# A decoder layer on one core: attention and expert stages joined in one block, row scores reordered, weight lows moved to VectorE, the routed tail sent by halves

## The chip, the cores and the metric

The kernel runs on one core of a Trainium2 chip. The metric is the device time of one execution in microseconds; the time of a kernel is the median over its runs. All times below come from one profiled execution, unless a median is named.

## What is computed

The input x has 8 sequences of 512 tokens with 256 features (4096 tokens in all), the context has 64 tokens per sequence. The layer does three things, each added to x:

```
x = x + mamba_like(layernorm(x))                 # its state input is constant: a fixed causal kernel
x = x + cross_attention(layernorm(x), ctx, ctx)  # 16 heads of 16, causal mask, softmax, output Wo
x = x + moe(layernorm(x))                        # shared MLP 256-1024-256 on all tokens, plus
                                                 # 8 experts of the same size, top 2 of 8 per token
```

The expert part in full:

```
shared = gelu(xf @ Wfc_s + bfc_s) @ Wproj_s + bproj_s
probs = softmax(xf @ Wr); keep the two largest, divide by their sum -> gate
routed = sum over e of (gelu(xf @ Wfc[e] + bfc[e]) @ Wproj[e] + bproj[e]) * gate[:, e]
```

## The kernel before, in words

The program is written by hand, engine by engine: each engine has its own list of instructions, which it takes strictly in order, and semaphores order them against each other. There are three blocks, and all engines meet at a barrier between two blocks. The first block is the mamba-like stage (to about 166 us). The second is attention (to about 371 us). The third holds the shared expert stage and the routed stage, which follow each other without a barrier.

A batch is one sequence: 512 tokens, four tiles of 128. A matmul in nearly full precision is three matmuls (`product`, lines 135 to 137): each operand is split into a high part (rounded by ScalarE) and a low part (whole minus high, `low`, line 141, on VectorE or GpSimd).

**Attention**, batch b of 8. For the softmax the row maxima are needed. `row_scores(b, t)` (L636) computes the scores of 128 queries for all heads into PSUM banks 4 and 5, and VectorE's `maxima(b, t)` (L903, L905) reduces them; as both banks are used for each tile, row scores t+1 wait for the maximum of t. `maxima_twice`, `transpose_maxima` (L656), `maxima_high` (ScalarE, L788) and `maxima_split` (VectorE, L914) bring the maxima into the layout of the keys. `key_scores(b, m)` (L664), for two halves m of the heads, computes transposed scores minus maxima; `exps` (ScalarE, L783) takes the exponentials; `weigh_values` (L682) sums them (L686) and weighs the values with them (L692). The sums are transposed (L696), inverted on VectorE (L919), spread over the features on ScalarE (L803) and transposed back (`spread_inverse`, L702); `divide` (VectorE, L924, L928) multiplies. Then `o_high` and `o_low` split the result, `project_o` (L709) multiplies by Wo, and `residual` (L935) adds to x. `project_q` (L627) makes the queries.

The work is pipelined over batches: while batch b has its key scores, batch b+1 has its row scores, batch b+2 its transposed input and queries, and batch b-1 its output projection. The order on TensorE is the loop at L739 to L766, that on VectorE L969 to L1007, that on ScalarE L826 to L849. The weights of the shared MLP are split here too: the high parts in four pieces on ScalarE (L839, batches 0 to 3), the low parts in two pieces on GpSimd (L871 to L875, beside batches 5 and 6 of its own list). GpSimd also computes the reciprocal standard deviations (L120, L122) and adds the bias of Wo to x (`add_bo`, L857 to L861). VectorE's normalisation of a batch (`apply_part`, L889 to L895) is four instructions.

**Shared stage**, batch b of 8: `transposes` (L1110), `logits` (L1130) and `transpose_logits` for the router, `choose` (VectorE, L1329) picks two experts by a chain of 14 short instructions, `ranks` counts the tokens before each, `place_rows`, `place_slots`, `place_gates` compute where a token's row goes, and GpSimd scatters the rows to DRAM (L1275). `up` (L1121) and `gelus` make the hidden layer, `lows` splits it, `down` (L1159) projects. TensorE's prologue for batch 0 is L1191 to L1198, then come whole batches. SP loads the router weights and biases at the start of the block (L1081 to L1084), GpSimd the weights of expert 0 (L1280).

**Routed stage**, blocks of 256 rows of one expert, 35 in the profiled execution: SP loads the rows, TensorE transposes, up and down, and at the end of a block VectorE adds the bias in both halves (`y`, L1633), multiplies both by the gate (L1638), and GpSimd adds both to the output by indirect transfers (L1599).

Of the kernel before, what the change touches and what calls it, by code (L numbers as in the profile page):

```python
# [18 lines left out]
def build(nc, d):  # L19
# [38 lines left out]
    with ctx:  # L58
# [110 lines left out]
        onesbd = ab("onesbd", [P, KD, PW])  # L169

# [391 lines left out]
        with ExitStack() as c:  # L562
# [18 lines left out]
            recs = used("recs", [P, KD, TB, P])  # L581
            causalT = tmp("causalT", [P, S])
            causalT16 = tmp("causalT16", [P, S], BF16)
            hTp_at = Place(hT_at)
# [6 lines left out]
                c, """b_hn_var b_hn_rstd b_hn_ready b_hT_psum b_hT_ready b_q_psum b_qT_ready b_bo_added b_n_psum  # L591
# [14 lines left out]
            with nc.Block() as block:  # L606
                @block.sync
                def _(sp):
                    sp.dma_start(selraw[:].rearrange("p m n -> p (m n)"), d["sel"]).then_inc(t_in, 16)
                    sp.dma_start(causalT[:], d["causalT"]).then_inc(t_in, 16)  # L610
                    sp.dma_start(fcraw[:], d["Wfc_s"].rearrange("(k p) e -> p k e", p=P)).then_inc(ws_in, 16)
                    sp.dma_start(prraw[:], d["Wproj_s"].rearrange("(k p) e -> p k e", p=P)).then_inc(ws_in, 16)

                @block.tensor
                def _(pe):
                    def transpose_x(b, i):
                        u = 2 * b + i
                        pe.wait_ge(hn_ready, TB * b + 2 * i + 2)
                        if u > 1:
                            pe.wait_ge(hT_ready, u)  # L620
                        for t in pair(i):
                            for k in range(KD):
                                last = nc.tensor.transpose(PS[:, x_bank(b, i), (k * 2 + t % 2) * P:(k * 2 + t % 2 + 1) * P],
                                                           hn[:, t, k * P:(k + 1) * P], ident[:])
                        last.then_inc(hT_psum, 1)

                    def project_q(b, m):  # L627
                        pe.wait_ge(hT_ready, 2 * b + 2)
                        if b:
                            pe.wait_ge(n_max, TB * b)  # L630
                        for k in range(KD):
                            last = product(PS[:, QB[m], :], [w[:, k, m * P:(m + 1) * P] for w in wqp],
                                           [x[:, k, :] for x in hTp], k == 0, k == KD - 1)
                        last.then_inc(q_psum, 1)

                    def row_scores(b, t):  # L636
                        i = TB * b + t
                        pe.wait_ge(qT_ready, KD * b + KD)
                        if i:
                            pe.wait_ge(n_max, i)  # L640
                        for m in range(KD):
                            for half in range(2):
                                rows = slice(half * P // 2, (half + 1) * P // 2)
                                at = PS[:, 4 + half, :].rearrange("p (i m n) -> p i m n", i=2, m=KD)[:, :, m, :]
                                last = nc.tensor.matmul(
# [3 lines left out]
                                if t and m == KD - 1:  # L649
                                    last.then_inc(n_psum, 1)  # L650
# [5 lines left out]
                    def transpose_maxima(b):  # L656
                        pe.wait_ge(mx_twice, b + 1)
                        if b > 1:
                            pe.wait_ge(x2_ready, 2 * (b - 1) - 1)
# [66 lines left out]
                    for m in range(KD):  # L726
                        project_q(0, m)
# [1014 lines left out]
```

## Time and profile before

| | us |
|---|---|
| median of 3 runs | 1019.85 (1019.09 to 1022.16) |
| the profiled execution, own time | 1017.67 |
| its span in the trace | 1015.8 |
| TensorE busy | 928.6 (91%), weight loads 794.4 (78%) |
| VectorE, ScalarE, GpSimd busy | 628.0 (62%), 556.8 (55%), 360.0 (35%) |
| mean granted TensorE clock | 0.982 of 2.4 GHz |
| chain that ended last, by engine | TensorE 58%, VectorE 2%, ScalarE 1%, transfers 1%, issue 1% |

The busy share is an average over stages with different limits. The chain that ended last names TensorE for most of what it covers. Where TensorE is busy all the time, only fewer or shorter matmuls would help; where it has gaps, the order of the work counts. The rows below are therefore read stretch by stretch.

### The profile page before, as it was taken

What the parts mean: (1) busy time and instruction counts of PE and PEld (TensorE: products, weight loads), DVE (VectorE), ACT (ScalarE), POOL (GpSimd) and SP (SyncE); (2) the same over time, 40 slices, a digit from 0 to 9 for tenths busy, and PEclk for the clock granted to TensorE, in tenths of its full rate; (3) what the DMA queues carried; (4) which work ended last, traced back from release to release, by engine and by line L of the source; (5) the groups of instructions that cost most, each with busy time, mean ns of one, the idle gap of its engine ahead of it and who ended that gap; (6) DMA issues with size and microseconds to landing.
All of it is one profiled execution on the core that took longest, in us unless ns stands there. A gap on an engine that the chain in (4) does not pass through costs nothing.

```text
span 1015.8 us, 20188 instructions
## 1 busy us (share of the span) xinstructions
PE 928.6 (91%) x6832; PEld 794.4 (78%) x6833; DVE 628.0 (62%) x1481; ACT 556.8 (55%) x1109; POOL 360.0 (35%) x325
## 2 busy tenths in 40 slices
PE   2998897789989767999999999999999999999995
PEld 2444696446556446888888989999999999999995
DVE  4898896766775537666665654656565655565552
ACT  2688752445445434555655456756576656566552
POOL 3641813221340016555555414323234332333222
PEclk9999899999999999999999999999999999999998
DMA  8200002000000012111112445422425242422322
GB/s 253 84 1 1 1 1 90 1 1 1 1 1 1 2 29 105 66 65 66 62 63 76 165 172 132 129 43 44 134 43 131 43 130 54 125 43 48 48 43 32
DMA packets 49312, 64.21 MB, mean 63 GB/s; under 512 B 10289, under 2 KB 42290, under 8 KB 49138
## 3 DMA queue, kind: packets, MB, share of 16 engines
q0 software_dynamic: 17504, 34.87, 14.5%
q1 hardware_dynamic: 31618, 27.68, 9.1%
q10 hardware_dynamic: 144, 1.05, 0.3%
q8 instruction: 28, 0.46, 0.2%
q14 instruction: 18, 0.15, 0.0%
HBM read 38.82 MB, written 24.77 MB: 63 GB/s over the span
## 4 chain that ended last, share of the span: by engine, by line
PE 58%; DVE 2%; ACT 1%; issue 1%; DMA 1%; SPq 0%; POOL 0%; DVEq 0%; POOLq 0%; ACTq 0%
PE PS L135 19%; PE PS L136 18%; PE PS L137 18%; PE PS L1525 2%; PE PS L1117 1%; DVE hidl L141 1%; DMA xr<-routed_rows 0%; ACT act L1214 0%; ACT hidh L1211 0%; PE PS L1142 0%; DVE wprl L141 0%; DVE wfcl L141 0%; POOL out_rows L1599 0%; PE PS L1151 0%; DMA wr<-in_Wr 0%
## 5 line engine op out<-in xcount | busy, mean ns | idle before, releaser
L1571 ACT ACTIVATE hideh<-PS,be 128x256 fp32r<-128x256 f32 x280 | 138.8, 496 | 148.1 <-PE PS L137 148.1
L1599 POOL DMA_INDIRECT out_rows<-y,toki x70 | 123.7, 1768 | 268.0 <-DVE y L1638 257.3
L141 DVE TENSOR_TENSOR hidel<-act32e,hideh 128x256 fp32r<-128x256 f32 x280 | 117.7, 425 | 95.6 <-ACT act32e L1573 95.3
L135 PE MATMUL PS<-xTeh,wfch 128*128 128x256 f32 x560 | 159.6, 285 | 1.2 <-issue 1.1
L137 PE MATMUL PS<-xTeh,wfcl 128*128 128x256 f32 x560 | 158.4, 283 | 0.0
L136 PE MATMUL PS<-xTel,wfch 128*128 128x256 f32 x560 | 158.4, 283 | 0.0
L135 PE MATMUL PS<-wprh,hideh 128*128 128x256 f32 x560 | 157.9, 282 | 0.0
L136 PE MATMUL PS<-wprl,hideh 128*128 128x256 f32 x560 | 154.9, 277 | 0.0
L137 PE MATMUL PS<-wprh,hidel 128*128 128x256 f32 x560 | 154.9, 277 | 0.0
L1573 ACT ACTIVATE act32e<-PS,be 128x256 f32<-128x256 f32 x280 | 139.0, 496 | 7.4 <-DVE hidel L141 7.0
L135 PEld LDWEIGHTS PS<-xTeh,wfch 128*128 128x128 f32 x560 | 107.2, 191 | 2.7 <-issue 1.9
L137 PEld LDWEIGHTS PS<-xTeh,wfcl 128*128 128x128 f32 x560 | 107.3, 192 | 0.0
L136 PEld LDWEIGHTS PS<-xTel,wfch 128*128 128x128 f32 x560 | 107.3, 192 | 0.0
L136 PEld LDWEIGHTS PS<-wprl,hideh 128*128 128x128 f32 x560 | 105.3, 188 | 0.0
L137 PEld LDWEIGHTS PS<-wprh,hidel 128*128 128x128 f32 x560 | 105.3, 188 | 0.0
L135 PEld LDWEIGHTS PS<-wprh,hideh 128*128 128x128 f32 x560 | 105.2, 188 | 0.0
L120 POOL TENSOR_TENSOR vare<-mv,small 128x4 f32<-128x4 f32 x24 | 9.5, 396 | 200.6 <-DVE mv L115 200.5
L1211 ACT ACTIVATE hidh<-PS,bfs 128x512 fp32r<-128x512 f32 x64 | 44.0, 688 | 59.4 <-PE PS L137 55.5
L1275 POOL DMA_INDIRECT routed_rows<-rows,slotc x64 | 67.2, 1050 | 24.6 <-issue 18.1
L135 PE MATMUL PS<-wpsh,hidh 128*128 128x256 f32 x256 | 73.5, 287 | 0.2 <-DVE hidl L141 0.2
L137 PE MATMUL PS<-wpsh,hidl 128*128 128x256 f32 x256 | 72.1, 281 | 0.0
L136 PE MATMUL PS<-wpsl,hidh 128*128 128x256 f32 x256 | 72.0, 281 | 0.0
(254 smaller groups left out, 2182.1 us busy)
## 6 DMA issues: line engine op xcount, KB each, us to landing
xr<-routed_rows SPq DMA_DIRECT2D x36, 272.0 KB, 2.7
fcraw<-in_Wfc POOLq DMA_DIRECT2D x8, 1024.0 KB
prraw<-in_Wproj POOLq DMA_DIRECT2D x8, 1024.0 KB
X<-in_x SPq DMA_DIRECT2D x8, 512.0 KB, 6.4
out_rows<-X SPq DMA_DIRECT2D x8, 512.0 KB, 3.0
routed_rows<-pads SPq DMA_DIRECT2D x8, 272.0 KB
out_rows<-y,toki POOLq DMA_INDIRECT x70, 3.8
ctx<-in_ctxT SPq DMA_DIRECT2D x4, 256.0 KB
```

The costliest lines, as they stand in the source:

```text
L120: nc.gpsimd.tensor_tensor(vare[:], mv[:, :, 1], eps4, ALU.add).then_inc(done, 1)
L135: nc.tensor.matmul(out, wh, xh, start=first, stop=False)
L136: nc.tensor.matmul(out, wh, xl, start=False, stop=False)
L137: return nc.tensor.matmul(out, wl, xh, start=False, stop=last)
L141: return eng.tensor_tensor(out, whole, high.bitcast(F32), ALU.subtract)
L1117: last = nc.tensor.transpose(PS[:, 4 + k, t * P:(t + 1) * P], hn[:, t, k * P:(k + 1) * P], ident[:])
L1211: nc.scalar.activation(hid[0][:, j, :], PS[:, j % 4, :], ACT.Gelu_apprx_tanh, bias=bfs[:, j:j + 1])
L1275: nc.gpsimd.indirect_dma_start(out=RG, out_offset=bass.IndirectOffsetOnAxis(ap=slotc[:, t, m:m + 1], axis=0), in_=rows[:, t, :], in_offset ...
L1525: last = nc.tensor.transpose(PS[:, 4, k * BLK + h * P:k * BLK + (h + 1) * P], xr[:, h, k * P:(k + 1) * P], ident[:])
L1571: nc.scalar.activation(hid[0][:, j, :], PS[:, j % 4, 0:BLK], ACT.Gelu_apprx_tanh, bias=bias)
L1573: nc.scalar.activation(act32[:, j % 2, :], PS[:, j % 4, 0:BLK], ACT.Gelu_apprx_tanh, bias=bias).then_inc(h_ready, 1)
L1599: nc.gpsimd.indirect_dma_start(out=out, out_offset=bass.IndirectOffsetOnAxis(ap=toki[:, h:h + 1], axis=0), in_=y[:, h, :], in_offset=None, ...
```

## The change

1. The attention stage becomes a set of functions that the last block calls: its engine lists stand in front of the shared stage's, in one block, and no barrier lies between them. The loops run over batches 0 to 6; batch 7 is written out among the shared prologue.
2. On TensorE, row scores 3 of batch b+1 stand behind `weigh_values(b)` (before: in front), `project_o(b-1, 0)` is cut into its two tiles with row scores, key scores and transposes between them, and `transpose_maxima` stands between the two `project_q`. `project_q(b, 0)` no longer waits for the maxima. ScalarE has `maxima_high` behind the spreads, between the two `evac_q`. VectorE has `invert_sums` in front of the normalisation and `residual(b-1, 0)` behind the second `x_low`.
3. The low parts of the shared MLP's weights are computed on VectorE, in four pieces of 1024 columns, behind `divide` of batches 1 to 4 (before: two pieces of 2048 on GpSimd).
4. At the end of a routed block the bias is multiplied by the gate first (`gated`), one instruction per half computes PSUM times gate plus that, and GpSimd sends each half when it is ready.
5. Many small tiles move so that they don't overlap with attention's; waits are added where tiles do overlap.

The diff, cut to its core (indentation changes left out):

```diff
+            def attention_tensor(pe):
                 def project_q(b, m):
                     pe.wait_ge(hT_ready, 2 * b + 2)
-                    if b:
+                    if m and b:
                         pe.wait_ge(n_max, TB * b)
-                def project_o(b, i):
+                def project_o(b, i, tiles=None, bank=YB):
                     pe.wait_ge(oT_ready, KD * b + KD)
-                    if u:
+                    if bank == YB:
                         pe.wait_ge(x2_ready, u)
-                    if i:
-                        pe.wait_ge(mx_ready, min(b + 3, B))
+                        pe.wait_ge(mx_ready, min(b + 2 + i, B))
...
-                for b in range(B):
+                for b in range(B - 1):
                     key_scores(b, 0)
                     row_scores(b + 1, 0)
                     transpose_x(b + 2, 0)
-                    project_o(b - 1, 0)
+                    project_o(b - 1, 0, [0])
                     row_scores(b + 1, 1)
                     key_scores(b, 1)
                     row_scores(b + 1, 2)
                     transpose_x(b + 2, 1)
-                    row_scores(b + 1, 3)
+                    project_o(b - 1, 0, [1])
                     weigh_values(b)
-                    transpose_maxima(b + 1)
+                    row_scores(b + 1, 3)
                     transpose_sums(b)
-                    for m in range(KD):
-                        project_q(b + 2, m)
+                    project_q(b + 2, 0)
+                    transpose_maxima(b + 1)
+                    project_q(b + 2, 1)
                     spread_inverse(b)
                     project_o(b - 1, 1)
-                for i in range(2):
-                    project_o(B - 1, i)
...
                 # ScalarE
                     evac_sums(b)
-                    maxima_high(b + 1)
                     evac_o(b)
                     for m in range(KD):
                         spread(b, m)
-                        evac_q(b + 2, m)
+                    evac_q(b + 2, 0)
+                    maxima_high(b + 1)
+                    evac_q(b + 2, 1)
...
                 # GpSimd
-                    if b in (5, 6):
-                        parts, whole = ((wfs, fcraw), (wps, prraw))[b - 5]
-                        low(nc.gpsimd, parts[1][:], whole[:], parts[0][:]).then_inc(ws_low, 1)
...
                 # VectorE
-                    residual(b - 1, 0)
                     stats_part(b + 3)
                     maxima(b + 1, 2)
                     x_low(b + 2, 1)
+                    residual(b - 1, 0)
                     maxima(b + 1, 3)
                     maxima_twice(b + 1)
+                    invert_sums(b)
                     for t in range(TB):
                         apply_part(b + 3, t)
                     maxima_split(b + 1)
-                    invert_sums(b)
                     divide(b)
+                    if 0 < b < 5:
+                        dve.wait_ge(ws_high, b)
+                        low(nc.vector, parts[1][:, part], whole[:, part], parts[0][:, part]).then_inc(ws_low, 1)
                     residual(b - 1, 1)
...
             def shared_sync(sp):
+                sp.wait_ge(att_s_psum, 2 * NG * (B - 1))
                 sp.dma_start(wr[:], d["Wr"].rearrange("(k p) e -> p k e", p=P)).then_inc(wr_in, 16)
...
                 # TensorE, prologue of the shared stage
+                key_scores(B - 1, 0)
                 transposes(0)
+                project_o(B - 2, 0)
+                key_scores(B - 1, 1)
                 logits(0)
-                up(0, range(2))
+                weigh_values(B - 1)
+                transpose_sums(B - 1)
+                project_o(B - 2, 1)
                 transpose_logits(0)
-                up(0, range(2, 4))
+                spread_inverse(B - 1)
+                up(0, range(2))
+                pe.wait_ge(att_o_divided, B)
+                up(0, range(2, 3))
+                project_o(B - 1, 0)
+                project_o(B - 1, 1, bank=6)
+                up(0, range(3, 4))
                 ranks(0)
+                pe.wait_ge(att_x2, 2 * B)
                 whole(0, 4)
...
                 # ScalarE
+                exps(B - 1, 0)
                 evac(0)
+                exps(B - 1, 1)
                 copy_rows(0)
-                act.wait_ge(w_in, W_IN)
                 evac_logits(0)
+                evac_sums(B - 1)
+                evac_o(B - 1)
+                spread(B - 1, m), for both m
+                act.wait_ge(w_in, W_IN)
+                o_high(B - 1, m), for both m
                 gelus(0, range(4))
...
                 # GpSimd
                 pool_wait(pool, w_in, W_IN)
+                pool_wait(pool, att_ws_low, TB)
                 load_weights(pool, 0)
+                pool_wait(pool, att_s_psum, 2 * NG * B)
                 nc.gpsimd.memset(pads[:], 0.0).then_inc(pads_zeroed, 1)
...
                 # VectorE
+                norm_apply(0).then_inc(hn_ready, 1)
+                o_low(B - 2, m), for both m
                 ... router weights, x_low(0)
+                att_residual(B - 2, 0)
                 stats_part(1)
-                lows(0, range(2))
+                invert_sums(B - 1)
+                att_residual(B - 2, 1)
+                divide(B - 1)
+                o_low(B - 1, m), for both m
                 choose(0)
+                att_residual(B - 1, 0)
+                lows(0, range(2))
+                att_residual(B - 1, 1, bank=6)
                 apply_part(1)
                 lows(0, range(2, 4))
                 place_rows(0)
...
+                dve.wait_ge(bias_added, TB * B)
                 low(nc.vector, wfc[1][:, 0], fcraw[:], wfc[0][:, 0]).then_inc(e_low, 1)
...
-            shared_done = (h_ready, KH * B + HELD)
+            shared_done = (y_psum, 2 * B)
...
                 # routed, GpSimd
-                        pool_wait(pool, y_ready, g * 2 + 2)
                         for h in range(2):
+                            pool_wait(pool, y_read, g * 2 + 3 + h)
                             nc.gpsimd.indirect_dma_start(
...
                 # routed, VectorE
                         for h in range(2):
-                            dve.wait_ge(y_psum, g * 2 + h + 1)
-                            nc.vector.tensor_tensor(y[:, h, :], PS[:, 5 + h, 0:D], bpr[e], ALU.add).then_inc(y_read, 1)
+                            last = nc.vector.tensor_scalar(gated[:, h, :], bpr[e], gate[:, h:h + 1], None, ALU.mult)
+                        last.then_inc(bias_gated, 1)
+                        dve.wait_ge(bias_gated, g + 1)
                         for h in range(2):
-                            dve.wait_ge(y_read, g * 2 + 3 + h)
-                            nc.vector.tensor_scalar(y[:, h, :], y[:, h, :], gate[:, h:h + 1], None, ALU.mult).then_inc(y_ready, 1)
+                            dve.wait_ge(y_psum, g * 2 + h + 1)
+                            nc.vector.scalar_tensor_tensor(y[:, h, :], PS[:, 5 + h, 0:D], gate[:, h:h + 1],
+                                                           gated[:, h, :], ALU.mult, ALU.add).then_inc(y_read, 1)
```

## Rows read from the trace of the kernel before

**Rows 1.** One line's instructions (the division): count, durations in ns, first and last start.

```profile
L928 DVE TENSOR_TENSOR oT<-oT,PS x8: 1220/1222/1222, 211.6 to 363.3; 128x1024 f32<-128x1024 f32 x8
```

**Rows 2.** Busy time by stretches from one division to the next, batches 2, 3, 5, 6, 7.

```profile
core 0: us, PE busy (x) PEld busy (x) DVE busy (x) ACT busy (x) POOL busy (x), PEclk, DMA share, GB/s
...
233.79:256.28 22.49, 20.31 (x161) 13.08 (x160) 14.75 (x27) 11.72 (x20) 3.98 (x6) 1.00 0.00 1
256.28:281.17 24.89, 22.15 (x161) 13.21 (x160) 18.53 (x26) 11.72 (x20) 8.49 (x7) 0.93 0.00 1
...
306.08:327.36 21.28, 20.30 (x161) 13.08 (x160) 11.36 (x15) 10.79 (x19) 0.00 (x0) 1.00 0.00 1
327.36:347.67 20.31, 16.65 (x141) 10.11 (x140) 11.76 (x20) 8.54 (x15) 1.22 (x2) 1.00 0.00 1
347.67:363.27 15.60, 11.70 (x103) 6.64 (x102) 5.71 (x10) 8.05 (x14) 0.00 (x0) 1.00 0.01 2
```

**Rows 3.** Timeline from batch 7 of attention to the logits of shared batch 1.

```profile
356.45 1.92 PE L686 MATMUL PS<-prT,onesbd 128*32 128x512 f32 x16 [2.07 <-ACT prT L786]
...
365.35 1.29 DVE L141 TENSOR_TENSOR oTl<-oT,oTh 128x512 fp32r<-128x512 f32 x2
...
371.06 0.69 DVE L939 TENSOR_TENSOR X<-X,PS 128x512 f32<-128x512 f32 x1 [1.87 <-PE PS L137]
...
383.48 0.18 DVE L1332 COPY lg<-PS 128x32 f32<-128x32 f32 x1
...
386.48 1.38 DVE L127 TENSOR_SCALAR hn<-X,mv,rstd 128x256 f32<-128x256 f32 x4
...
394.60 0.39 PE L135 MATMUL PS<-xT1h,wrh 128*8 128x512 f32 x1 [1.29 <-DVE xT1l L141]
```

**Rows 4.** Timeline of batch 2: start us, length us, engine, line, operation, idle time before.

```profile
242.76 2.06 ACT L786 ACTIVATE prT<-PS 128x512 f32<-128x512 f32 x4 [3.33 <-PE PS L679]
...
246.53 1.13 PE L645 MATMUL PS<-kbd,qT 64*128 64x256 f32 x8 [2.07 <-DVE mxpad L905]
...
247.59 1.92 PE L686 MATMUL PS<-prT,onesbd 128*32 128x512 f32 x16
247.71 1.22 DVE L905 TENSOR_REDUCE mxpad<-PS 128x16 f32<-128x1024 f32 x1 [0.73 <-PE PS L645]
...
251.17 0.66 PE L661 MATMUL PS<-ident,mxpad 128*128 128x128 f32 x4
...
251.86 0.60 ACT L790 ACTIVATE mxh<-PS 128x512 fp32r<-128x512 f32 x1 [1.68 <-PE PS L661]
...
252.49 0.75 DVE L916 SCALAR_TENSOR_TENSOR mxT<-mxh,small,PS 128x512 fp32r<-128x512 f32 x1 [1.53 <-ACT mxh L790]
```

**Rows 5.** Timeline: normalisation and bias addition in batch 2, GpSimd's low in batch 3, VectorE's later one.

```profile
246.82 2.79 POOL L861 TENSOR_TENSOR X<-X,bo 128x256 f32<-128x256 f32 x4
...
249.59 1.37 DVE L894 TENSOR_SCALAR hn<-X,mv,rstd 128x256 f32<-128x256 f32 x4
...
271.78 4.57 POOL L141 TENSOR_TENSOR wfsl<-fcraw,wfsh 128x2048 fp32r<-128x2048 f32 x1
271.80 5.67 DVE L894 TENSOR_SCALAR hn<-X,mv,rstd 128x256 f32<-128x256 f32 x4
...
571.35 2.28 DVE L141 TENSOR_TENSOR wfcl<-fcraw,wfch 128x2048 fp32r<-128x2048 f32 x1
```

**Rows 6.** DMA issues: KB and us from issue to landing.

```profile
bpr<-in_bproj ACTq DMA_DIRECT2D x1, 1024.0 KB, 8.2
```

**Rows 7.** One tile's instructions (y), the line of its sums.

```profile
L1633 DVE TENSOR_TENSOR y<-PS,bpr x70: 414/424/426, 603.3 to 1004.6; 128x256 f32<-128x256 f32 x70
```

**Rows 8.** Timeline behind the last matmul (which ends at 1004.5).

```profile
1004.57 0.42 DVE L1633 TENSOR_TENSOR y<-PS,bpr 128x256 f32<-128x256 f32 x1 [2.19 <-PE PS L137]
1004.91 0.61 DVE L1638 TENSOR_SCALAR y<-y,gate 128x256 f32<-128x256 f32 x2
1006.32 1.55 POOL L1599 DMA_INDIRECT out_rows<-y,toki  x1 [8.12 <-DVE y L1638]
1008.18 1.55 POOL L1599 DMA_INDIRECT out_rows<-y,toki  x1 [0.30 <-issue]
```

More of the change, by code:

```diff
@@ L559, in _, with attention_stage @@
                     norm_rstd(pool, hn_rstd, 2 * B)
[L562 removed]
+        def attention_stage():
             tmp = Place(kbd_at + 4 * B * KD * HG * S)
@@ new lines, in attention_gpsimd, with rstds, add_bo @@
+            def attention_gpsimd(pool):
+                def rstds(i):
+                    pool_wait(pool, hn_var, i + 1)
+                    norm_rstd(pool, hn_rstd, 2 * i)
+                def add_bo(b):
+                    pool_wait(pool, hn_ready, TB * b + TB)
+                    for t in range(TB):
+                        xs = X[:, TB * b + t, :]
+                        nc.gpsimd.tensor_tensor(xs, xs, bo[:], ALU.add).then_inc(bo_added, 1)
+                pool.sem_inc(hn_rstd, 2)
+                rstds(1)
+                nc.gpsimd.memset(mxpad[:], 0.0).then_inc(mx_zeroed, 1)
+                add_bo(0)
+                for b in range(1, B):
+                    if b + 1 < B:
+                        rstds(b + 1)
+                    add_bo(b)
+                rstds(B)
@@ L1015, in build @@
+            return ((attention_sync, attention_tensor, attention_scalar, attention_gpsimd, attention_vector),
+                    (s_psum, o_copied, o_divided, x2_ready, ws_low, hn_rstd, hT_psum), NG, bps_at, late_at)
+        attention, att, NG, bps_at, late_at = attention_stage()
+        att_s_psum, att_o_copied, att_o_divided, att_x2, att_ws_low, att_hn_rstd, att_hT_psum = att
         with ExitStack() as c:
@@ L1245, in shared_scalar @@
                 act.sem_inc(h_ready, HELD)
+                exps, evac_sums, evac_o, spread, o_high = attention[2](act)
+                exps(B - 1, 0)
                 evac(0)
+                exps(B - 1, 1)
                 copy_rows(0)
+                evac_logits(0)
+                evac_sums(B - 1)
+                evac_o(B - 1)
+                for m in range(KD):
+                    spread(B - 1, m)
                 act.wait_ge(w_in, W_IN)
-                evac_logits(0)
+                for m in range(KD):
+                    o_high(B - 1, m)
                 gelus(0, range(4))
@@ L1655, in _ @@
                 def _(sp):
+                    attention[0](sp)
                     shared_sync(sp)
```

766 lines of the change are left out of this document (372 added, 394 removed).

## The prediction

> **What bounds the kernel now.** The table above gives TensorE 91% of the span; the question is where the other 9% stands. I cut the span at the division of each attention batch (L928), which ends a batch. Eight divisions lie between 211.6 and 363.3 [rows 1]; the stretches between them [rows 2] show three things. Batch 2 takes 22.49 us with TensorE busy for 20.31; batch 3 takes 24.89 though its work is the same; batches 5, 6 and 7 take 21.28, 20.31 and 15.60. Batches 1 and 4, by difference from the 151.7 us of [rows 1], take 47.1 together (22.2 and 24.9 in the same view). Behind the last division lies a stretch in which TensorE has little to do until the logits of shared batch 1 start at 394.60 [rows 3]; from there to the end it is almost never idle. So time can be won before 394.60, or in the tail behind the last matmul, and hardly elsewhere.
>
> **Why a batch takes 22.5 us.** Row scores 3 start at 246.53 after TensorE sat idle for 2.07 us, waiting for a maximum on VectorE [rows 4]. The value matmuls stand behind them, at 247.59, though their exponentials had ended at 242.76 + 2.06 = 244.8. From 247.59 to the division all is TensorE work: 3.6 us of value matmuls (to 251.17), transposes, query projection, inverse, output projection.
>
> **Order of row scores.** I lay the new order out from the start of a batch's key scores (0). Key scores and row scores 0 end at 3.0, a quarter of the output projection at 4.1; row scores 1 wait for the first maximum until 4.6 and end at 5.7; key scores, row scores 2, transposes and the second quarter end at 9.4, where the exponentials (2.06 from 7.2) are just done. Values to 13.0, row scores 3 to 14.1, sums 14.5, query projection 15.9, maxima transposed 16.4, second query projection 17.8, inverse 19.1. Beside this runs the chain that the new order lengthens: row scores 3 at 13.0, maximum from 14.2 to 15.4 (1.2 behind, 1.22 long), copy 0.2, inversion 0.55, then on ScalarE two spreads, a query evacuation and only then the maxima, four of 0.60 to 0.67 (the row at 251.86), then 0.75 on VectorE: 19.4 [rows 4]. The last output projection waits for that (0.4) and ends the batch at 21.1. VectorE divides beside it, so key scores wait for nothing more. Batch 2 gains 1.4, batch 1 gains 1.1, batch 5 gains 0.2. Batch 6 has no query projection to cover the longer chain: 20.4, a loss of 0.1. Batch 0 gains 0.3.
>
> **Weight lows.** In batch 3 GpSimd subtracts 2048 columns in 4.57 us, and VectorE's four normalisations take 5.67 beside it, 1.37 without it [rows 5]. The 4.3 us delay maxima_split and lengthen batches 3 and 4 by 2.4 us each over batch 2; removed, each comes to 21.1 as well: 3.8 + 3.8. The lows return as four of half the size on VectorE, at 2.28/2 = 1.14 us each [rows 5], after the division of batches 1 to 4. VectorE waited 1.23 us there in the old timeline for the first maximum, so I count 0; with no such cover it would be 4 x 1.14 = 4.6. Attention in sum: 0.3 + 1.1 + 1.4 + 3.8 + 3.8 + 0.2 - 0.1 = **10.5**. From below 4.8 (only GpSimd's interference goes), from above 14.6 (every batch falls to batch 2's 20.3 us of TensorE's busy time [rows 2]). I take 10.5, since both chains above were laid out step by step.
>
> The rows show that a GpSimd operation holds up VectorE for its whole length. The Trainium skill, "SBUF — State Buffer", section "Who interferes with whom", says that these two share a pair of ports under an exclusive lock, and that a VectorE instruction with two SBUF inputs contends with a GpSimd one that reads SBUF. That speaks against the change: the new lows have two such inputs. GpSimd's bias additions are 2.79 us for four [rows 5], so four meetings would cost 4 x 0.7 = 2.8 by that rule; these additions start 13 us behind the previous division and the lows 1.2 behind one, so the sum with or without the rule is the same unless they drift together.
>
> **One block.** Before: from the division of batch 6 (347.67) to logits 1 (394.60) 46.9 us [rows 2, 3]. In it batch 7 runs alone, ends with two projections and residuals, then a barrier, a load of the router weights that everybody awaits, and the shared prologue with its choice of experts. After, from the start of key scores 7 (1.5 behind that division): normalisation (1.4), transposes 0, projection and second key scores come before the value matmuls at 9.1 (before: 356.45 - 349.0 = 7.4); 6.9 to the division at 16.0 (before 363.27 - 356.45 = 6.8; a projection fills TensorE's wait for the spreads); division 1.2, ScalarE's highs and two lows 1.29 to 19.1; choice of experts 3.0 (383.48 to 386.48) to 22.1; residual 0.69, two lows, residual to 24.6; from the normalisation of batch 1 to logits 1 8.1 as before (386.48 to 394.60): 32.7 [rows 3]. With the 1.5 that is 34.2, so **12.8** less. This chain is VectorE's; TensorE has some 26 us of work in it: 11.7 busy to the division of batch 7 [rows 2], and projections and up parts of some 14 behind it. From above the gain is therefore 20.7; from below 5, if the 8 us of matmuls on this chain (values 3.6, two projections, key scores) ran at half the clock.
>
> Waits added: SP's for the key scores of batch 6 is over 13 us before batch 7, and behind it stand only four small loads. GpSimd takes the expert loads next, then the bias additions and rstd of batch 1, some 5 us in all, wanted only at 24.6. VectorE's wait for bias additions of batch 7 is met two batches earlier. ScalarE's load of bpr now follows the last down projection; it takes 8.2 us [rows 6] beside a first routed block of 11.6 (34.5 blocks from the first to the last of 70 sums, 603.3 to 1004.6 [rows 7]), so 0; if late, a microsecond or two, once.
>
> **Tail.** The last half's sum starts at 1004.57 (0.42), two multiplications end at 1005.52, GpSimd's sends start at 1006.32 and 1008.18 [rows 8]. After, the first half is sent beside the matmuls of the second, one fused operation ends at 1005.0, and the last send starts 0.8 behind, at 1005.8: **2.4** less. From below 0.5 (VectorE's part alone). The fused operation reads PSUM like the sum; I give it 0.42 to 0.45. The gatings move ahead of VectorE's wait for TensorE (2.19 at 1004.57) and cost nothing.
>
> **Sum.** 10.5 + 12.8 + 2.4 = 25.7. The profiled execution took 1017.67 (span 1015.8 and 1.9 around it): 992.0. The median shown, 1019.85, lies 2.2 above it, so the forecast is **994.2**.
>
> **Rivals.**
> 1. The order gives nothing, only GpSimd's interference goes: 4.8 + 12.8 + 2.4 = 20.0, 999.9. For it: in my layout the maxima chain ends 0.4 us behind TensorE's own work, so whatever is late on it lengthens every batch. Against: the wait of 2.07 us in each of batches 1 and 2 has no cause left. Chance 0.2.
> 2. The block is joined, but the prologue doesn't overlap as it reads, because TensorE runs at 1.2 GHz in it: 10.5 + 5 + 2.4 = 17.9, 1002. For it: the granted clock, a mean over its levels of 1.2 and 2.4 GHz, was 0.93 in batch 3, in which TensorE had paused [rows 2]. Against: TensorE is busier there than before. The Trainium skill, "TensorE: Matmul & The Clock Gate", section "What's actually happening", makes the slow state the default that activity releases; by it the new order should rather gain clock. Chance 0.15.
> 3. TensorE alone bounds attention, and half of what is left in the joined part goes too: 14.6 + 16.5 + 2.4 = 33.5, 986. Against: both chains end in real dependencies. Chance 0.1.
> 4. Slower: in each routed block the gatings and the wait on them stand ahead of the sums, so y_read comes late and TensorE waits at its down projection. There are 35 blocks (70 sums [rows 7], two in each); it takes 0.74 us in each to cancel 25.7, and 0.83 to be slower by over 0.3%. Against: 2.19 us of idle time in front of the sum. At 1 us each: 1029. Chance 0.03; a smaller stall that ends within 0.3% has 0.02.
>
> The forecast has 0.5. The range reaches over rivals 1, 2 and most of 3: gains of 31 to 18, **989 to 1002**. What this kernel's runs can tell from no change is about 0.3%, 3 us. Faster 0.95, same 0.02, slower 0.03.
>
> **What would show it.** Divisions some 21 us apart from batch 1 to 5, and no normalisation of several us; value matmuls right behind the exponentials; TensorE's wait before the last projection of a batch under 1 us; logits of batch 1 near 371 instead of 394.60, 34 behind the division of batch 6; routed blocks still 11.6 us apart; last send 1.3 us behind the last matmul. I am wrong if batches stay at 22 us, if logits 1 come over 40 us behind that division, or if TensorE waits for y_read.

## The result and the profile after

| | before | after |
|---|---|---|
| median, 4 runs each on one chip | 1019.47 (1017.22 to 1022.16) | 993.41 (989.96 to 996.28) |
| ratio, 95% interval | | 0.9724 [0.9687, 0.9761] |
| profiled execution, its span | 1017.67, 1015.8 | 989.96, 988.3 |
| mean granted clock | 0.982 | 0.987 |

Faster by 26.1 us in the medians; forecast were 25.7 and a time of 994.2. The profiled execution of after is the fastest of its four, 3.5 below their median, so in the profiles the difference is 27.7. The stages below are compared by their own intervals, which hardly move from run to run; what does move are the start of attention (division 0 between 208 and 212 in the kernels of this study) and the way from the shared stage into the routed one.

The division line and the windows from one division to the next, as in [rows 1, 2]; the page's line on the chain that ended last.

```profile
L920 DVE TENSOR_TENSOR oT<-oT,PS x8: 1212/1214/1221, 210.4 to 353.0; 128x1024 f32<-128x1024 f32 x8
...
210.43:230.99 20.56, 18.68 (x146) 11.61 (x146) 13.29 (x26) 11.72 (x20) 3.99 (x6) 1.00 0.00 1
230.99:252.03 21.04, 20.29 (x158) 13.05 (x158) 15.06 (x29) 11.73 (x20) 4.00 (x6) 1.00 0.00 1
252.03:273.06 21.03, 20.29 (x158) 13.05 (x158) 14.93 (x28) 11.73 (x20) 4.00 (x6) 1.00 0.00 1
...
294.09:315.13 21.04, 20.29 (x158) 13.05 (x158) 12.26 (x17) 10.79 (x19) 1.25 (x2) 1.00 0.00 1
315.13:335.35 20.22, 17.26 (x138) 10.04 (x138) 11.54 (x21) 8.54 (x15) 3.15 (x4) 1.00 0.26 84
335.35:353.02 17.67, 16.04 (x132) 9.93 (x133) 10.15 (x33) 10.41 (x18) 4.55 (x7) 1.00 0.11 35
...
PE 71%; DVE 7%; ACT 3%; issue 1%; DMA 0%; POOL 0%; SPq 0%; DVEq 0%; POOLq 0%; ACTq 0%
```

Batches 2 to 5 all take 21.04 us or 0.01 less. TensorE's busy time is what it was in batch 2 [rows 2]; only its idle time has shrunk, from 2.2 us to 0.75. Batch 3's normalisation is no longer slow (1.28 us, the last row of the next block; 5.67 in [rows 5]) and its clock is 1.00. The batch at the joint takes longer than before (17.67, not 15.60), with 16.0 us of TensorE work in it instead of 11.7: the shared prologue lies inside it.

The timeline of batch 2, to be held against [rows 4], and as last row the normalisation in batch 3.

```profile
232.12 1.22 DVE L141 TENSOR_TENSOR wfsl<-fcraw,wfsh 128x1024 fp32r<-128x1024 f32 x1
...
240.04 2.07 ACT L783 ACTIVATE prT<-PS 128x512 f32<-128x512 f32 x4 [2.95 <-PE PS L680]
...
242.39 1.92 PE L687 MATMUL PS<-prT,onesbd 128*32 128x512 f32 x16
...
245.96 1.13 PE L646 MATMUL PS<-kbd,qT 64*128 64x256 f32 x8
...
250.75 0.59 ACT L787 ACTIVATE mxh<-PS 128x512 fp32r<-128x512 f32 x1
251.22 0.69 ACT L777 ACTIVATE qT<-PS,bq 128x512 f32<-128x512 f32 x1
251.36 0.75 DVE L908 SCALAR_TENSOR_TENSOR mxT<-mxh,small,PS 128x512 fp32r<-128x512 f32 x1 [1.08 <-ACT mxh L787]
...
252.26 0.36 PE L135 MATMUL PS<-woh,oTh 128*128 128x256 f32 x1 [0.49 <-DVE mxT L908]
...
270.04 1.28 DVE L886 TENSOR_SCALAR hn<-X,mv,rstd 128x256 f32<-128x256 f32 x4
```

Values start 0.28 us behind the exponentials (242.11), not 2.8. Row scores 3 follow them, waiting for nothing. What is left of TensorE's waits is the row at 252.26: the last projection waits 0.49 us for the split maxima.

The joint, held against [rows 3], and the tail, against [rows 8].

```profile
369.71 0.40 PE L135 MATMUL PS<-xT1h,wrh 128*8 128x512 f32 x1 [1.02 <-DVE xT1l L141]
...
976.64 0.48 DVE L1673 SCALAR_TENSOR_TENSOR y<-PS,gate,gated 128x256 f32<-128x256 f32 x1 [0.33 <-PE PS L137]
...
977.93 1.55 POOL L1633 DMA_INDIRECT out_rows<-y,toki  x1 [7.39 <-DVE y L1673]
979.36 0.48 DVE L1673 SCALAR_TENSOR_TENSOR y<-PS,gate,gated 128x256 f32<-128x256 f32 x1 [2.23 <-PE PS L137]
980.65 1.55 POOL L1633 DMA_INDIRECT out_rows<-y,toki  x1 [1.17 <-DVE y L1673]
```

Logits 1 start 34.36 us behind division 6 (335.35), before 46.93. The first half is sent at 977.93, while TensorE still works on the second. The span of 27.5 us less is made of four pieces: to division 6 12.32 (347.67 - 335.35), from there to logits 1 12.57, from logits 1 to the last matmul 0.3, behind it 2.29 (11.26 to 8.97).

### The profile page after: what moved, and what is told of

Same layout as the page of the kernel before. It is cut to its first block, busy times and chain, and to the rows that moved or that the text cites. A ratio compares the mean times of both kernels' runs of the same rounds, so it can differ in the third digit from the quotient of the medians.

```text
span 988.3 us, 20180 instructions
## 1 busy us (share of the span) xinstructions
PE 923.4 (93%) x6832; PEld 792.9 (80%) x6833; DVE 625.2 (63%) x1485; ACT 556.4 (56%) x1109; POOL 347.0 (35%) x323
## 4 chain that ended last, share of the span: by engine, by line
PE 71%; DVE 7%; ACT 3%; issue 1%; DMA 0%; POOL 0%; SPq 0%; DVEq 0%; POOLq 0%; ACTq 0%
PE PS L135 20%; PE PS L136 19%; PE PS L137 19%; PE PS L646 3%; DVE mxpad L897 2%; PE PS L1559 2%; PE PS L687 2%; PE PS L673 2%; PE PS L693 1%; ACT recs L802 1%; ACT prT L783 1%; PE PS L1109 1%; DVE mxT L908 1%; DMA xr<-routed_rows 0%; DVE hidl L141 0%
## 5 line engine op out<-in xcount | busy, mean ns | idle before, releaser
L1291 POOL DMA_INDIRECT routed_rows<-rows,slotc x64 | 65.5, 1024 | 24.9 <-issue 19.3
```

The source lines that it names most:

```text
L1291: nc.gpsimd.indirect_dma_start(out=RG, out_offset=bass.IndirectOffsetOnAxis(ap=slotc[:, t, m:m + 1], axis=0), in_=rows[:, t, :], in_offset ...
```

## The experiments

D0 to D7 are the eight divisions; the values that compare stages come from one profiled execution of each kernel. A dip is a stretch in which TensorE's granted clock is below 1.00. "D0 to D6" is 136.11 us in before and 124.92 in after.

### The order and the lows, one at a time (e1, e2, e3)

e2 is before with the lows moved to VectorE, nothing else:

```diff
                         divide(b)
+                        if 0 < b < 5:
+                            dve.wait_ge(ws_high, b)
...
+                            low(nc.vector, parts[1][:, part], whole[:, part], parts[0][:, part]).then_inc(ws_low, 1)
...
-                            low(nc.gpsimd, parts[1][:], whole[:], parts[0][:]).then_inc(ws_low, 1)
```

> The kernel before with one part of the change: the low parts of the shared weights on VectorE, four pieces behind the division of batches 1 to 4, none on GpSimd. My theory: only GpSimd's interference goes, so the divisions of batches 3 and 4 come 22.5 us behind the ones before (24.9 before) and the whole is 4.8 us shorter; batches 1 and 2 stay at 22.2 and 22.5. Rival: the four pieces of 1.14 us lie on the path on VectorE, which gives 4.6 back: no change, batches 1 to 4 each 1.1 longer than they would be.

Measured 1017.83 beside 1021.3, ratio 0.9965 [0.9938, 0.9992]; D0 to D6 134.69, so 1.4 less, not 4.8. Windows of batches 2, 3, 4 of e2, and three rows of its batch 3:

```profile
233.78:256.28 22.50, 20.28 (x161) 13.07 (x160) 15.76 (x27) 11.72 (x20) 4.00 (x6) 1.00 0.00 1
256.28:280.15 23.87, 21.93 (x161) 13.28 (x160) 15.29 (x27) 11.72 (x20) 3.97 (x6) 0.93 0.00 1
280.15:304.02 23.87, 21.94 (x161) 13.29 (x160) 15.32 (x28) 10.78 (x19) 6.76 (x10) 0.93 0.01 1
...
268.76 1.47 PE L645 MATMUL PS<-kbd,qT 64*128 64x256 f32 x8 [1.81 <-DVE mxpad L900]
270.16 3.23 PE L686 MATMUL PS<-prT,onesbd 128*32 128x512 f32 x16
271.80 1.37 DVE L889 TENSOR_SCALAR hn<-X,mv,rstd 128x256 f32<-128x256 f32 x4
```

The normalisation is back at 1.37 us: GpSimd's interference is gone, as I had it. But both batches stand at a granted clock of 0.93: behind TensorE's pause of 1.81 us the sums take 3.23 us instead of 1.92. The batches are 1.4 us longer than batch 2. Its batch 6, too, took 20.95 at 0.96, where before has 20.31. In before, batch 3 had the same 0.93 and batch 4 had 1.00, and both took 24.9 (the first in [rows 2]): the dip cost nothing there, since the late normalisation held the batch anyway.

The 1.4 is therefore no fixed price. The dips differ between executions of the same attention code: e4 (below), whose attention is that of before, has them in batches 2 and 3:

```profile
233.09:257.22 24.13, 21.78 (x160) 13.29 (x160) 14.57 (x27) 11.72 (x20) 3.97 (x6) 0.93 0.00 1
257.22:282.09 24.87, 22.00 (x160) 13.21 (x160) 18.67 (x26) 11.72 (x20) 8.48 (x7) 0.93 0.00 1
```

By the whole times (10 runs of e2, 13 of before) the lows alone are worth 3.5 us, with an interval of 0.8 to 6.3, in which both 1.4 and 4.8 lie.

e3 is before with the new order alone (part 2 of the change, within the old attention block), e1 is after with the lows back on GpSimd:

```diff
# e1
+                        low(nc.gpsimd, parts[1][:], whole[:], parts[0][:]).then_inc(ws_low, 2)
...
-                        low(nc.vector, parts[1][:, part], whole[:, part], parts[0][:, part]).then_inc(ws_low, 1)
```

> The kernel before with another part alone: the new order of attention's steps on all engines, weight lows still on GpSimd, separate blocks, old tail. My theory: batches 1 and 2 take 21.1 us; in batches 3 and 4 GpSimd's 4.57 us now meet the copy of the maxima, which stands just in front of their transposes, so they take about 23.4 instead of 24.9; from the first division to that of batch 6 5.5 to 6 us less than the 136.1 before. Rival 1 of the prediction: the order gives nothing, 136.1 stays.

> The changed kernel with the weight lows back on GpSimd as two whole pieces. My theory: two batches rise from 21.0 to about 23.4, 4.6 us more in all. Rival (the parts just add up, as without the new order): 2.4 a batch as in the kernel before, 4.8. If the new order hides GpSimd's operation: under 1.

e3: 1011.09, ratio 0.9909 [0.9887, 0.993], D0 to D6 128.81. e1: 993.67, ratio 0.9755 [0.9716, 0.9793], D0 to D6 128.80. Windows of batches 2 to 4 in e3, and GpSimd's low with its neighbours on VectorE in e1:

```profile
231.14:252.16 21.02, 20.28 (x158) 13.04 (x158) 13.95 (x27) 11.71 (x20) 3.99 (x6) 1.00 0.01 1
252.16:275.14 22.98, 20.51 (x158) 12.98 (x158) 15.89 (x27) 11.71 (x20) 8.49 (x7) 1.00 0.00 1
275.14:298.13 22.99, 20.51 (x158) 12.98 (x158) 15.90 (x27) 10.78 (x19) 10.06 (x10) 1.00 0.01 1
```

```profile
264.75 4.54 POOL L141 TENSOR_TENSOR wfsl<-fcraw,wfsh 128x2048 fp32r<-128x2048 f32 x1
...
265.94 1.23 DVE L902 TENSOR_REDUCE mxpad<-PS 128x16 f32<-128x1024 f32 x1 [3.20 <-PE PS L646]
267.20 2.14 DVE L909 COPY mxpad<-mxpad 128x64 f32<-128x64 f32 x1
...
269.73 1.28 DVE L891 TENSOR_SCALAR hn<-X,mv,rstd 128x256 f32<-128x256 f32 x4
```

The four corners of D0 to D6: 136.1 (before), 134.7 (lows alone), 128.8 (order alone), 124.9 (both). Lows alone give 1.4 in the old order and 3.9 in the new one; the order gives 7.3 with GpSimd's lows and 9.8 without. In these executions the two parts are worth more together than the sum of each alone (11.2 against 8.7): in batches 3 and 4 of the old order a dip lay under the late normalisation, and removing that uncovered it. All of this surplus hangs on e2's dips. Without them (1.37 in each of two batches, 0.64 in batch 6) e2 would stand at an estimated 131.3, the lows alone at 4.8, and the parts would nearly add up (12.1 against 11.2). The order's own worth doesn't hang on them: 7.3 with GpSimd's lows in place, and by the whole times 9.3 us, 7.1 to 11.5. In e1 GpSimd's low meets another instruction than in before: the 128x64 copy waits with it (2.14 us; 0.39 in batch 3 of before), the normalisation comes behind and is whole at 1.28; the batch pays 1.95. The whole times of e1 and after (0.9755 and 0.9724) have overlapping intervals; it is the divisions that show the 3.9.

### Are the lows on VectorE free (e7)

```diff
+                        link(low(nc.vector, parts[1][:, part], whole[:, part], parts[0][:, part]))
                         low(nc.vector, parts[1][:, part], whole[:, part], parts[0][:, part]).then_inc(ws_low, 1)
```

> The changed kernel with each of the four weight lows on VectorE computed twice (the second waits for the first). VectorE waits about 1.0 us for the first maximum of a batch, so the single low is covered but a second of 1.2 us is not quite. Theory: batches 1 to 4 rise by 0.1 to 0.4 each, 0.5 to 1.5 us in all. Rival (the lows lie on the path): 1.2 each, 4.9 in all.

993.52, ratio 0.9726 [0.9686, 0.9766]. Batches 2 to 5 take 21.28 us, 0.25 over after; a second low is 1.2 us of work. So the cover holds for most of a second low. That the first costs nothing is seen in e3: its batch 2 has no low on either engine and takes 21.02 us, after's with one takes 21.04.

### Which piece of the order (e8, e12, e9)

```diff
# e8: after, row scores 3 ahead of the values again
+                    row_scores(b + 1, 3)
                     weigh_values(b)
-                    row_scores(b + 1, 3)
# e12: after, projection and residual where they were
-                        project_o(b - 1, 0, [0])
+                        project_o(b - 1, 0)
...
-                        project_o(b - 1, 0, [1])
...
                     maxima(b + 1, 1)
+                    if behind:
+                        residual(b - 1, 0)
...
                         x_low(b + 2, 1)
-                    if behind:
-                        residual(b - 1, 0)
```

> The changed kernel with row scores 3 in front of the value matmuls again, all else as changed. Theory A (the stall of 2.07 us came from this place alone): batches rise from 21.0 to about 22.3, some 7 us in all. Theory B (moving the residual behind the second low on VectorE brought the second-last maximum forward by 0.7, and the chain of the maxima is now relieved by as much as the wait costs): 21.4 a batch, 2 us in all.

> The kernel after with one piece of its order undone: project_o(b-1, 0) whole ahead of row scores 1, and residual(b-1, 0) on VectorE behind the second maximum, as before; row scores 3 stay behind the value matmuls. Theory A (the residual and two lows ahead of the third maximum are what made TensorE wait, so that this piece is the gain): batches go back towards 22 to 22.5. Theory B (the two moves cover each other: with row scores 3 behind the values, a late third maximum is hidden by 3.6 us of value matmuls; with the residual moved it isn't late; each alone suffices): batches 1 to 4 at 21.0 to 21.3, division 0 to division 6 at 124.5 to 126.

e8: 991.91, ratio 0.9727 [0.9697, 0.9757], batches 1 to 5 20.95, 21.18, 20.95, 20.96, 20.64, D0 to D6 124.41. e12: 992.11, ratio 0.972 [0.9683, 0.9757], batches 1 to 5 20.71, 21.18, 21.18, 21.18, 21.18, D0 to D6 125.66. TensorE in batch 2 of e8, where the wait of 2.07 us [rows 4] had been:

```profile
244.35 1.13 PE L646 MATMUL PS<-kbd,qT 64*128 64x256 f32 x8 [0.70 <-DVE mxpad L897]
245.41 1.92 PE L687 MATMUL PS<-prT,onesbd 128*32 128x512 f32 x16
```

Undoing either piece alone costs next to nothing: D0 to D6 is 0.5 shorter in e8 and 0.7 longer in e12 than in after, and the whole times don't differ. They are two cures of one wait: with the residual behind the third maximum, that maximum is early; with row scores 3 behind the values, a late one is covered by 3.6 us of value matmuls. That undoing both would bring back the batch of 22.5 us is likely but not shown: no run has the old places of both within the new order. My account of the gain named row scores 3 alone.

e9 is after with ScalarE's copy of the maxima ahead of the first query evacuation:

```diff
-                    if after:
-                        evac_q(b + 2, 0)
                     maxima_high(b + 1)
                     if after:
-                        evac_q(b + 2, 1)
+                        for m in range(KD):
+                            evac_q(b + 2, m)
```

> The changed kernel with one swap on ScalarE: the copy of the maxima stands in front of both query evacuations instead of between them. TensorE waits about 0.4 us in each batch for the maxima before its last output projection. Theory: that wait goes, divisions 20.65 us apart instead of 21.04 in batches 1 to 5, some 2 us in all. Rival: the division waits for the transposed inverse anyway, or the later query evacuation holds up TensorE: no change or slower.

991.53, ratio 0.9709 [0.9677, 0.9741]; batches 1 to 5 take 20.41 and four times 20.45, D0 to D6 122.00. Window of batch 2 of e9, and the end of that batch:

```profile
232.23:252.68 20.45, 20.03 (x159) 13.05 (x160) 15.14 (x27) 11.72 (x21) 4.00 (x6) 1.00 0.00 1
...
251.59 0.75 DVE L907 SCALAR_TENSOR_TENSOR mxT<-mxh,small,PS 128x512 fp32r<-128x512 f32 x1 [0.50 <-ACT mxh L787]
...
252.48 0.36 PE L135 MATMUL PS<-woh,oTh 128*128 128x256 f32 x1
```

The wait of 0.49 us ahead of the last projection is gone and batches 2 to 5 are 0.59 shorter each. That shows what bounded after: the chain of the maxima, which the prediction had laid out as 0.4 us too long.

### The joint (e5, e6)

e5 keeps one block but finishes attention before the prologue of the shared stage starts; e6 puts the barrier back as well, and the router load behind it:

```diff
# e5, TensorE (ScalarE's and VectorE's lists likewise)
                 key_scores(B - 1, 0)
-                transposes(0)
                 project_o(B - 2, 0)
                 key_scores(B - 1, 1)
-                pe.wait_ge(wr_split, 2)
-                logits(0)
                 weigh_values(B - 1)
...
                 project_o(B - 1, 0)
-                project_o(B - 1, 1, bank=6)
+                project_o(B - 1, 1)
+                transposes(0)
+                pe.wait_ge(wr_split, 2)
+                logits(0)
...
# e6: as e5, and
+            with nc.Block() as block:
+                @block.sync
+                def _(sp):
+                    shared_sync(sp)
```

> The changed kernel, still one block without a barrier, but with batch 7 finished as before (its two projections and residuals included) before the shared prologue starts in its old order. Between the division of batch 6 and the logits of shared batch 1 lay 46.9 us before and 34.4 in the changed kernel. Theory: the gain is the overlap of the two chains, so this kernel takes about 45.5 here (only the barrier and the router load, some 1.4 us, are saved), 11 us more than the changed one. Rival: the barrier, with what stands behind it, is what cost: 40 us or less.

> As the one before, but with the barrier between attention and the shared stage back, and the router load behind it. Theory: 46.9 us between the division of batch 6 and logits 1, as in the kernel before, 12.5 us more than the changed kernel. Rival: more than 2 us over the kernel without the barrier.

e5: 1004.35, ratio 0.9835 [0.9797, 0.9872], D6 to logits 1 44.74. e6: 1006.9, ratio 0.9867 [0.9828, 0.9906], D6 to logits 1 49.66. Windows of e6 (D6 to D7, to the barrier, to the first low of the hidden part, to logits 1), then the second and third of these for before:

```profile
333.04:349.17 16.13, 11.94 (x103) 6.92 (x104) 5.70 (x12) 8.05 (x14) 0.00 (x0) 1.00 0.00 2
349.17:358.96 9.79, 5.99 (x36) 5.24 (x34) 4.54 (x6) 1.15 (x2) 0.00 (x0) 0.75 0.00 0
358.96:369.59 10.63, 8.21 (x27) 5.29 (x27) 4.18 (x21) 5.17 (x7) 5.40 (x8) 0.59 0.39 137
369.59:382.70 13.11, 7.89 (x45) 5.99 (x44) 11.49 (x40) 6.09 (x11) 5.53 (x7) 0.87 0.18 64
```

```profile
363.27:371.75 8.48, 4.67 (x36) 4.09 (x34) 4.54 (x6) 1.15 (x2) 0.00 (x0) 1.00 0.00 0
371.75:381.80 10.05, 7.19 (x31) 4.55 (x32) 4.17 (x21) 5.28 (x8) 4.58 (x7) 0.83 0.39 110
```

e6 has the structure of before here, and takes 2.7 us more. Most of it goes with a lower granted clock around the barrier (0.75 and 0.59 where before has 1.00 and 0.83): in these two windows e6 is 1.9 us longer and TensorE's busy time 2.3. Of the joint's gain, the overlap is 44.74 - 34.36 = 10.4 us. What the barrier costs lies between 2.2 (before's 46.93 less e5's 44.74) and 4.9 (e6's 49.66 less 44.74), depending on the clock that TensorE is granted behind it. e3, which has the barrier and the new order too, lies between with 47.48, 2.7 more than e5. Why the clock fell further in e6 than in before, with nearly the same pauses of TensorE, isn't shown.

### The tail and the gatings (e4, e10)

e4 is before with part 4 of the change alone (its diff is the two last hunks of the change's).

> The kernel before with the tail alone: bias gated first, one fused operation per half, each half sent when ready. Theory: from the end of the last matmul to the end of the span 9.0 us instead of 11.3, and nothing else changes (blocks 11.6 us apart): 2.3 us less. Rival: only VectorE's shorter part counts, 0.5 less.

1019.37, ratio 0.9988 [0.996, 1.0017]. From the last sum to the end of the span 8.9 us, before 11.2: the 2.3 us are there. The gatings in front of the sums cost nothing by themselves: from the first to the last of the 70 sums it takes 401.4 us, before 401.3. But its batch 2 took 24.13 us at clock 0.93, and logits 1 to the first routed sum 211.3 (208.7 in before): such scatter, a few us in each kernel, hides the tail in the whole time.

e10 adds eight gatings of the same kind, into tiles that nobody reads, to each routed block of after:

```diff
+                        for gx in gxs:          # four tiles
+                            for h in range(2):
+                                nc.vector.tensor_scalar(gx[:, h, :], bpr[e], gate[:, h:h + 1], None, ALU.mult)
                         for h in range(2):
                             last = nc.vector.tensor_scalar(gated[:, h, :], bpr[e], gate[:, h:h + 1], None, ALU.mult)
```

> The changed kernel with four more pairs of gatings (8 operations of about 0.31 us, 2.4 us, into tiles that nobody reads) in front of the sums in each routed block: a test of rival 4 of the prediction, in which what stands in front of the sums on VectorE makes TensorE wait. VectorE waits 2.2 us for the second half. Theory: blocks stay 11.6 us apart, only the tail grows by about 0.2 to 0.6 us. Rival 4: up to 2.4 us in each of 35 blocks, 20 to 80 us more.

1010.82, ratio 0.9894 [0.9846, 0.9942]. From the first to the last of the 70 sums 416.1 us, in after 400.3. Windows of e10 early and late in the routed stage, then the lines of the view of waits, 620 to 960 (engine, tile and line that waited, who released it: us in total, times, longest), then one such place in its timeline:

```profile
620.00:660.00 40.00, 37.36 (x320) 37.16 (x320) 29.55 (x87) 21.23 (x56) 13.68 (x9) 1.00 0.39 93
930.00:970.00 40.00, 40.00 (x342) 39.87 (x342) 26.42 (x78) 23.52 (x64) 12.41 (x8) 1.00 0.29 45
...
PE PS L135 <- ACT act32e L1608: 12.3, 6, 2.6
ACT act32e L1608 <- DVE hidel L141: 24.5, 16, 3.7
...
793.53 0.88 DVE L1679 SCALAR_TENSOR_TENSOR y<-PS,gate,gated 128x256 f32<-128x256 f32 x2
794.32 2.28 DVE L141 TENSOR_TENSOR wprl<-prraw,wprh 128x2048 fp32r<-128x2048 f32 x1
...
796.97 0.47 ACT L1608 ACTIVATE act32e<-PS,be 128x256 f32<-128x256 f32 x1 [3.08 <-DVE hidel L141]
797.50 0.39 PE L135 MATMUL PS<-xTeh,wfch 128*128 128x256 f32 x1 [1.99 <-ACT act32e L1608]
```

In after, TensorE has no such wait in that view, and ScalarE's comes to 2.0 us. So 2.4 us more on VectorE in each of 35 blocks (four times the 0.61 of a pair) cost 15.8 us in all, 0.45 per block, where I expected nothing (the kernels without it lie between 400.2 and 402.2, so at least 13.9). The last row shows the way: the sums are late, behind them stands the low of the next expert's weights (2.28), behind that the lows of the hidden part; ScalarE's second GELU waits for those, and TensorE for ScalarE. The last blocks, with no weights to split, keep their pace.

### A version beyond both (e11)

e9, and on VectorE two moves at the joint:

```diff
+                place_rows(0)
                 lows(0, range(2, 4))
-                place_rows(0)
...
                 def whole(b, first=2):
+                    x_low(b + 1)
                     if b == 0:
                         for m in range(2):
                             place_slots(0, m)
                         place_gates(0)
-                    x_low(b + 1)
```

> The kernel after with the copy of the maxima ahead of the first query evacuation (as in the run before of that name), and two more moves on VectorE at the joint with the shared stage: place_rows(0) ahead of the lows of hidden parts 2 and 3, and x_low(1) ahead of place_slots(0) and place_gates(0). Theory (the joined prologue is still VectorE's chain: TensorE waits 3.01 us at the transposes of batch 1 for the carry, and 1.02 at the logits for xT1l, which stands behind 14 placing instructions): transposes of batch 1 start 1.2 earlier, xT1l starts when ScalarE has copied, logits of batch 1 come 31.5 to 32.5 us behind the division of batch 6 (34.3 before), batches keep 20.45, the time is 988 to 990, some 2 under the kernel with the copy alone. Rival (the placing then stands late itself and TensorE waits for the next batch's ranks or hidden lows instead): the interval from logits 1 to the first routed sum grows by the same 2 us and the time stays at 991.5.

988.6 (5 runs, 986.07 to 991.36), ratio 0.9687 [0.9661, 0.9714]. TensorE's transposes of shared batch 1 in after and in e11:

```profile
364.62 1.88 PE L1109 MATMUL PS<-ident,hn 128*128 128x128 f32 x8 [3.01 <-DVE carry L1382]
```

```profile
362.01 1.32 PE L1108 MATMUL PS<-ident,hn 128*128 128x128 f32 x8 [1.80 <-DVE carry L1381]
...
365.69 0.58 PE L135 MATMUL PS<-xT1h,wrh 128*8 128x512 f32 x1
```

D6 to logits 1 is 31.72 us (34.33 in e9), logits 1 to the first routed sum 211.6 (211.4 in e9): the 2.6 us are kept. Its median is the lowest of the study, though the interval of its ratio still touches that of e9; the firm evidence is the joint.

## Why the prediction was right, step by step

The sum came out at 25.7 against 26.1 in the medians, for mostly the reasons given; one term was 1.8 too small and one reason was half of the truth. That the medians agree to 0.4 is partly luck: between the profiled executions the difference is 27.7, and 1.1 of that is the place of division 0.

- **Attention, 10.5.** Measured 12.3 to division 6. Batches 2, 3, 4, 5 gain 1.45, 3.86, 3.88, 0.24, forecast 1.4, 3.8, 3.8, 0.2: the layout of one batch, 21.1 long, came out at 21.04. Batch 1 was mis-sized (1.67, not 1.1): with less work than the others it takes 20.56. Batch 6 gains 0.09 (forecast -0.1). Batch 0 gains 1.13, not 0.3; as division 0 moves by 4 us between kernels, that isn't the change's to claim.
- **Order of row scores.** That the wait has no cause left was right, though it is 2.07 us only in batch 2; in batches 1, 3 and 4 it is 1.8. The new place of row scores 3 is only one of two sufficient causes of its going (e8, e12). The chain of the maxima was laid out correctly, and its 0.4 us are the bound of the new batch (a wait of 0.49; without it e9's batches are 0.59 shorter).
- **Weight lows.** They are free on VectorE (e3 beside after; e7). Ascribing 2.4 us in each of batches 3 and 4 to GpSimd was right in before's trace, but removing it alone gave 1.0 each in e2's profiled execution, with both batches at a granted clock of 0.93; the prediction had no term for that. Rival 1 (the order gives nothing, 20.0 in sum) is refuted by e3, where the order alone gives 7.3; its term of 4.8 is not, since e2's whole times allow it. The port rule that I weighed against the change never came to decide: the low stands at 232.12, the bias additions some 11 us later. What the rule says otherwise is borne out: by the Trainium skill, "SBUF — State Buffer", section "Who interferes with whom", a VectorE copy or tensor_scalar can contend for the pair and a tensor_reduce can't; beside GpSimd's low the copy took 2.14 us and the normalisation 5.67 [rows 5], the maxima 1.23 as ever.
- **One block, 12.8.** Measured 12.57. The chain is VectorE's, as laid out: logits 1 34.36 behind division 6, forecast 34.2. e5 and e6 split it: 10.4 overlap, at least 2.2 barrier and router load. From the normalisation of batch 1 to logits 1 it is 8.1 us, as forecast. TensorE's work in this stretch was put too low, at 26 us: it is 28.7 (16.0 to division 7, 12.7 behind it), so it idles for 5.7 us, and 4.0 of that are two waits for VectorE, for the carry and for xT1l. Rival 2 fell: the clock was 1.00 in batch 7 and 0.90 from there to logits 1.
- **Tail, 2.4.** Measured 2.29. The fused operation takes 0.48 us, not 0.42 to 0.45; the last send starts 1.3 behind the last matmul, as forecast. The 0 for the gatings held (e4). I had 2.19 us of idle time as cover for it; e10 shows that a further 2.4 us of it costs 0.45 per block. So rival 4's mechanism is real, and within 2.4 us of VectorE's work in each block; it bites through the hidden lows and ScalarE, not at y_read.
- **Rival 3** (TensorE alone bounds, 986) was reached in neither stage by after; e9 and e11 go part of that way.

## What to carry to other kernels

Lay out one period of a pipelined loop instruction by instruction on all engines, from measured durations: that gave 21.1 for 21.04, and named the next bound before it was there. Two causes of idle time in one place need not be additive: test each removal in both settings before giving it a price, and see first whether the granted clock was the same in the stretches compared. Before undoing or crediting a single move, ask whether another move of the same change covers the same wait.

## What the runs showed of the hardware

- In the old order TensorE pauses 1.8 to 2.1 us for a maximum in each batch from 1 to 4, and the granted clock of single batches fell, in different ones from kernel to kernel: 0.93 in batch 3 in before, 0.93 in 3 and 4 and 0.96 in 6 in e2, 0.93 in 2 and 3 in e4. A batch at 0.93 took 1.4 to 1.6 us longer, or nothing where the late normalisation held it. Other batches with the same pauses had 1.00, so the pause alone doesn't decide it. In the new order the longest pause up to division 6 is 1.6 us (once, in batch 1; 0.5 in batches 2 to 5 of after), and all eleven kernels with it show 1.00 in every window from division 0 to 6. What ties the dips to the pauses is this coincidence; no run changes the pauses alone. The Trainium skill, "TensorE: Matmul & The Clock Gate", section "What's actually happening", has activity release the slow state; the direction agrees.
- The dips show in whole times too: over the 44 runs of before beside the experiments, the mean granted clock ranges from 0.983 down to 0.969, and the times from 1017.39 (at 0.982) to 1027.99 (at 0.969). The runs of the kernels with the new order have 0.978 to 0.989.
- One GpSimd instruction of 4.5 us stretched a copy of 64 columns on VectorE from 0.39 to 2.14 us (e1), and another of 4.57 us the four normalisations from 1.37 to 5.67 us (before); a reduction out of PSUM beside it kept its 1.23 (e1).
